# Layer 1 of a gated cross-attention kernel: rows, normed rows and weighed products turned by transposing DMAs instead of TensorE

## The chip, the cores and the metric

One core of a Trainium2 chip runs the whole program. The metric is the device time of one execution in microseconds, as the median of several runs.

## The reference

```python
x = x + tanh(g_xattn[0]) * L0_xattn(layernorm(x), ctx)
x = x + tanh(g_ffn[0])   * L0_ffn(layernorm(x))            # 8 experts, top 2
x = x + tanh(g_xattn[1]) * L1_xattn(layernorm(x), ctx)
x = x + tanh(g_ffn[1])   * L1_ffn(layernorm(x))

def L1_xattn(x, c):        # 16 heads of 64
    q, k, v = x @ Wq / 8, c @ Wk, c @ Wv
    return softmax(q @ k.T) @ v @ Wo

def L1_ffn(x):             # 32 prototypes, rank 16
    dists = sqrt(max(|x|^2 + |p|^2 - 2 x @ prototypes.T, 0))
    w = softmax(-dists / max(|temp|, 0.1))
    topw, topi = top_k(w, 2);  topw = topw / sum(topw)
    return sum over both: topw * (A[topi] @ (B[topi] @ x) + bias[topi])
```

`x` is 64 x 256 x 256, the context 64 x 77 x 256, both f32. Everything from the third line of the sum on is "layer 1" here.

## The kernel before

The program prepares keys and values, runs layer 0's attention, layer 0's experts on the first 1024 rows, and then layer 1 in `attention_ffn_phase`. Only this last phase changes. It goes through 64 batches (`NB`) of 256 rows, two tiles of 128 rows each (`TPB`), so 128 tiles. Each matrix product in f16 is made of three matmuls, by `matmul3`: high x high, high x low, low x high. A high half is a ScalarE copy to f16 and a low half is a VectorE subtraction from the f32 value (`split_hi`, `split_lo`).

Each engine runs the same `body(i, u, j)` for batch i, with two iterations h, one per tile t = 2i + h. It is a software pipeline written out by hand: an iteration does the scores of tile t, the exp of t-1, the normalising of t-2, the turning of probabilities and the attention product of t-3, the second norm `yn` of t-4, the products `low` (with the prototypes' distances) of t-5, the weights of t-6, and the weighing `hw`, its turning and the last product `ffn` of t-7. `LAG` is 7: SyncE stores tile t-7 in iteration t. The queries of batch i+1 are made in four groups (`prep`) inside batch i, and its normed rows `xn` were made at the end of batch i-1.

TensorE's order in an iteration: turn the probabilities' group 0; group 1; the 48 score matmuls; group 2; in the first tile turn `xn` (four turns of 128x128 in f32); turn `hw` (four); `low` (12); turn `wsel`; the attention product (30 matmuls); a group of queries (12 matmuls); turn `yn` (two); `ffn` (13). All PSUM results but the scores go through five banks in a fixed ring (`Ring`, `uses`, `freed`); an entry of it waits for the reader of the entry five before.

VectorE's order: the sums' reciprocals; low halves of the probabilities; low half of `xnT` in the first tile; maxima of the scores; statistics of the rows two batches ahead; low half of `hwT`; the shifted scores; distances; the residual; `bn_stats`; a query's low half; averages `mv2`; `pick`; low half of `ynT`; `wsel`; the two nearest prototypes; the last addition to `y`.

GpSimd's order: in the second tile `deviation` (four steps on [128, 2]: add eps, negate the mean, a power of -0.5, a product); `deviation2` for tile t-4 (the same on [128, 1]); `weigh`; `length2` (three steps); `top_weights` (eight small steps, three of them powers); `normalise` (two products that write `pn`); `softmax_sums` (three adds).

SyncE issues every load and store of the phase in one order, and waits in that order. For a batch these are the keys (308 KB), the rows `x` (256 KB), two loads and two stores of a tile (128 KB each), and the values: two loads `vo_front` and eight `vo_back` of 13 partitions each.

Of the kernel before, what the change touches and what calls it, by code (L numbers as in the profile page):

```python
# [708 lines left out]
def attention_ffn_phase(nc, ctx, psum, const, src, src_rows, dst, keys, values, wq, score_scale, ffn, experts):  # L709
# [27 lines left out]
    VALUE_LOADS = 16 * (2 + MAIN)  # L737
# [6 lines left out]
    LAG = 7  # L744
# [3 lines left out]
    SUM_STEPS, LN2_STEPS, TOP_STEPS = 2, 2, 5  # L748
# [7 lines left out]
    xnT = pair("xnT", [P, DC, SEQ])  # L756
# [4 lines left out]
    idle, numbers = sb("idle", [P, 1]), sb("numbers", [P, 5])  # L761
# [17 lines left out]
    xnT_hi, xnT_ready, q_hi, q_ready = sem("xnT_hi"), sem("xnT_ready"), sem("q_hi"), sem("q_ready")  # L779
# [6 lines left out]
    ln2_sums, ln2_stats, ln2_step, ln2_done, ysq_done, yn_ready = (  # L786
        sem("ln2_sums"), sem("ln2_stats"), sem("ln2_step"), sem("ln2_done"), sem("ysq_done"), sem("yn_ready"))
    ln2_inverse = sem("ln2_inverse")
    ynT_hi, ynT_ready, dots_read = sem("ynT_hi"), sem("ynT_ready"), sem("dots_read")
# [4 lines left out]
    low_ready, hw_ready, hwT_hi, hwT_ready, wselT_hi, wselT_ready, out_ready = (  # L794
        sem("low_ready"), sem("hw_ready"), sem("hwT_hi"), sem("hwT_ready"), sem("wselT_hi"), sem("wselT_ready"),
# [33 lines left out]
    def norm_apply(i, u):  # L829

        need(act, ln_done, i + 1)
        for a in range(TPB):
# [27 lines left out]
    class First:  # L860
# [29 lines left out]
        def scalar_rows(self):  # L890
            act.wait_ge(early_full, 1)
            act.activation(xnT[0][:, :, :], parted(rows_bank, DC), ACT.Copy).then_inc(xnT_hi, 1)

        def vector_rows(self):
            dve.wait_ge(xnT_hi, 1)
            nc.vector.tensor_tensor(xnT[1][:, :, :], parted(rows_bank, DC), xnT[0][:, :, :], ALU.subtract)\
                .then_inc(xnT_ready, 1)

        def tensor_rows_taken(self):
            pe.wait_ge(xnT_ready, 1)  # L900

        def tensor_query(self, n):
            need(pe, q_ready, n - 1)
            for b in range(QB):
                at = (n * QB + b) * P
                for c in range(DC):
                    last = matmul3(nc, query_bank(n)[:, b * SEQ:(b + 1) * SEQ], [w[:, c, at:at + P] for w in wq],
                                   [a[:, c, :] for a in xnT], c == 0, c == DC - 1)
# [16 lines left out]
    k_sb.append(sb("k1", [P, BLK, KEYS, 2], F16))  # L925
    vo_front = [sb(f"vo_front{p}", [P, MAIN, 2, D], F16) for p in range(2)]
# [13 lines left out]
    ynT = pair("ynT", [P, DC, P])  # L940
# [10 lines left out]
    hwT = pair("hwT", [P, LC, P])  # L951
# [4 lines left out]
    def prep_uses(h, part):  # L956

        at = {(0, 1): [("xnT", 0)], (0, 2): [("q", 0)], (0, 3): [("q", 1)], (1, 0): [("q", 2)], (1, 2): [("q", 3)]}
        return at.get((h, part), [])

    def uses(i):

        names = []
        for h in range(TPB):
# [6 lines left out]
            names += prep(1)  # L971
            names += of(7, [("hwT", h)])
# [4 lines left out]
            names += of(4, [("ynT", h)])  # L977
            names += of(7, [("ffn", h)])
# [5 lines left out]
    def freed(i, use):  # L984
# [7 lines left out]
        if what == "xnT":  # L992
            return xnT_ready, i + 2
# [4 lines left out]
        if what == "ynT":  # L998
            return ynT_ready, t - 3
        return {"hwT": hwT_ready, "wselT": wselT_ready, "ffn": out_ready}[what], t - 6  # L1000
# [16 lines left out]

    def prob_of(u, h, age):
# [4 lines left out]
    last_keys = lambda tile: tile[:, H * FRONT:SC].rearrange("p (h k) -> p h k", h=H)  # L1023
# [5 lines left out]
    def _(sp):  # L1029
# [11 lines left out]
        def load_values(i, u, j):  # L1041
# [4 lines left out]
            for n in range(MAIN):  # L1046
                sp.dma_start(vo_back[p][n * BACK:(n + 1) * BACK, :, :, :], values_back(batch_at(i), n)).then_inc(vo_in[p], 16)
# [5 lines left out]

        def body(i, u, j):
            if live(i + 1, NB):
                load_keys(i + 1, *ahead(u, j, 1))
            for h in range(TPB):
                t = i * TPB + h - LAG
                if live(t, NT):
# [3 lines left out]
                if live(i * TPB + h - 2, NT):  # L1063
                    load_rows(i * TPB + h - 2, *place(2, u, h, j))
                if h == 0 and live(i + 3, NB):
                    load_x(i + 3, *ahead(u, j, 3))
# [21 lines left out]
    def _(pool):  # L1088
# [15 lines left out]
        def normalise(t, h, u):  # L1104
# [4 lines left out]
            for keys_of, first, end in ((first_keys, 0, FRONT), (last_keys, FRONT, KEYS)):  # L1109
                last = pool.tensor_tensor(keys_of(pn[h]), e[:, :, first:end],  # L1110
                                          rsum[h][:, :].unsqueeze(2).broadcast_to([P, H, end - first]), ALU.mult)
            last.then_inc(pn_ready, 1)

        def deviation2(t, h):

            need(pool, ln2_stats, t + 1)
            need(pool, yn_ready, t)
            step = Steps(pool, ln2_step, t, LN2_STEPS)
            vare_ready = pool.tensor_tensor(vare2[:, :], mv2[:, 1:2], eps[:, :], ALU.add)
            pool.tensor_scalar(minus_mean2[:, :], mv2[:, 0:1], -1.0, None, ALU.mult)  # L1120
            step(vare_ready)
            step(pool.tensor_tensor(rstd2[:, :], vare2[:, :], numbers[:, 0:1], ALU.pow))
# [1773 lines left out]
```

## Time and profile before

| what | value |
|---|---|
| median of 3 runs | 3064.41 us (3062.23 to 3066.16) |
| the profiled execution's own time | 3063.96 us |
| its span, first to last instruction | 3062.1 us |
| mean granted TensorE clock | 0.977 |
| busy in the span: TensorE, VectorE | 2839.0 us (93%), 2538.6 us (83%) |
| busy in the span: GpSimd, ScalarE | 2160.7 us (71%), 1832.1 us (60%) |
| first and last score maximum of layer 1 begin at | 1469.0 us, 2997.0 us |

An engine's busy time is the time that at least one of its instructions covers; matmuls overlap one another, so their pace is read from their starts and not from their durations. In a row of the timeline the first number is the start in microseconds from the span's start, the second the length.

### The profile page before, as it was taken

The page shows a single profiled execution, that of the slowest core. Times are in us where ns is not written, and L with a number is a line of the kernel's source. Part 1 is how long each engine was busy: PE and PEld are TensorE (multiplying, and loading weights), DVE is VectorE, ACT ScalarE, POOL GpSimd, SP SyncE. Part 2 cuts the span into 40 slices and gives each one's busy share as a digit, 9 for nine tenths or more (in the row PEclk, how much of TensorE's full clock was granted, in tenths as well). Part 3 has the DMA queues.
Part 4 walks back from the last instruction along what each step waited for, and adds up shares of the span by engine and source line. Part 5 has one row for each costly group of instructions (what it writes and reads, how often), then busy time and mean ns, then how long its engine had stood idle before and what let it go on. Part 6 is the DMA issues. An engine that isn't in the chain of part 4 may idle for free.

```text
span 3062.1 us, 98061 instructions
## 1 busy us (share of the span) xinstructions
PE 2839.0 (93%) x32554; PEld 2276.5 (74%) x32554; DVE 2538.6 (83%) x6189; ACT 1832.1 (60%) x3605; POOL 2160.7 (71%) x3859
## 2 busy tenths in 40 slices
PE   4888896899999999789899999999999999999997
PEld 2444444677777877557688888888888888888886
DVE  6877786788888888675799999899888899998986
ACT  2666765678777777575455555555555555555553
POOL 3893000666676666554599888888888888888887
PEclk7999998899999999899999999999999999999999
DMA  5987666233232333631544444444444444444431
GB/s 151 363 338 293 240 242 259 68 83 91 79 93 76 90 83 82 236 97 42 121 105 110 115 97 102 97 95 97 106 92 105 99 98 101 95 97 106 104 89 44
DMA packets 367616, 388.73 MB, mean 127 GB/s; under 512 B 118432, under 2 KB 341264, under 8 KB 362320
## 3 DMA queue, kind: packets, MB, share of 16 engines
q1 hardware_dynamic: 346960, 335.42, 39.5%
q0 software_dynamic: 7328, 23.40, 2.5%
q10 hardware_dynamic: 12960, 25.23, 2.2%
q8 instruction: 203, 3.33, 0.5%
q14 instruction: 165, 1.35, 0.2%
HBM read 235.08 MB, written 148.83 MB: 125 GB/s over the span
## 4 chain that ended last, share of the span: by engine, by line
PE 40%; DVE 6%; issue 3%; POOL 2%; ACT 1%; DVEq 0%; POOLq 0%; ACTq 0%
PE banks L150 11%; PE banks L152 11%; PE banks L151 11%; PE banks L1308 3%; PE banks L1293 2%; DVE a_probT_lo L1395 1%; PE banks L1340 1%; DVE a_pick L1518 1%; ACT a_qT_hi L1197 1%; DVE a_y L1537 1%; DVE a_rsum L1407 1%; DVE a_wsel L1527 0%; PE banks L1363 0%; PE banks L1355 0%; ACT a_ynT_hi L1197 0%
## 5 line engine op out<-in xcount | busy, mean ns | idle before, releaser
L1197 ACT ACTIVATE a_qT_hi<-banks 128x512 f16<-128x512 f32 x252 | 150.5, 597 | 692.5 <-PE banks L152 692.5
L383 POOL TENSOR_TENSOR a_probT_lo<-a_expT,a_probT_hi 128x512 f16<-128x512 f32 x256 | 291.3, 1159 | 218.9 <-ACT a_probT_hi L466 218.9
L459 ACT ACTIVATE a_expT<-banks,a_top,w_score_scale 128x512 f32<-128x512 f32 (+1 forms) x384 | 272.5, 710 | 153.5 <-PE banks L550 145.4
L1110 POOL TENSOR_TENSOR a_pn<-a_prob,a_rsum 128x1024 f32<-128x1024 f32 (+1 forms) x256 | 310.2, 1233 | 4.5 <-DVE a_rsum L1409 4.3
L150 PE MATMUL banks<-a_xnT_hi,w_q_hi 128*128 128x256 f16 x1024 | 280.8, 274 | 4.7 <-DVE a_xnT_lo L1393 3.0
L150 PE MATMUL banks<-a_vo_front,a_probT_hi 128*128 128x256 f16 x1024 | 279.2, 273 | 2.7 <-DVE a_probT_lo L1395 2.6
L152 PE MATMUL banks<-a_xnT_hi,w_q_lo 128*128 128x256 f16 x1024 | 280.2, 274 | 0.0
L151 PE MATMUL banks<-a_xnT_lo,w_q_hi 128*128 128x256 f16 x1024 | 280.1, 274 | 0.0
L152 PE MATMUL banks<-a_vo_front,a_probT_lo 128*128 128x256 f16 x1024 | 279.2, 273 | 0.0
L151 PE MATMUL banks<-a_vo_front,a_probT_hi 128*128 128x256 f16 x1024 | 279.1, 273 | 0.0
L1395 DVE SCALAR_TENSOR_TENSOR a_probT_lo<-banks,a_probT_hi 128x512 f16<-128x512 f32 (+1 forms) x384 | 212.1, 582 | 34.8 <-ACT a_probT_hi L1197 33.5
L1393 DVE TENSOR_TENSOR a_qT_lo<-banks,a_qT_hi 128x512 f16<-128x512 f32 x252 | 172.5, 684 | 69.9 <-ACT a_qT_hi L1197 66.2
L550 PE MATMUL banks<-ident,a_shifted 128*128 128x128 f32 (+1 forms) x1280 | 204.3, 283 | 5.3
L1197 ACT ACTIVATE a_probT_hi<-banks 128x512 f16<-128x512 f32 (+1 forms) x384 | 193.7, 523 | 25.1 <-PE banks L1308 25.1
L2264 DVE SCALAR_TENSOR_TENSOR kv_vo_out<-banks,kv_vo_out 128x512 f16<-128x512 f32 (+1 forms) x312 | 191.3, 679 | 15.3 <-ACT kv_vo_out L2162 15.3
L1308 PE MATMUL banks<-ident,a_pn 128*128 128x128 f32 (+1 forms) x1280 | 196.9, 277 | 2.4 <-issue 2.4
L659 DVE TENSOR_TENSOR a_shifted<-banks,a_smax 128x1024 f32<-128x1024 f32 (+1 forms) x256 | 192.1, 792 | 3.8
L2162 ACT ACTIVATE kv_vo_out<-banks 128x512 f16<-128x512 f32 (+1 forms) x312 | 172.4, 601 | 26.5 <-DMA vo<-kv_vo_out 20.1
L649 DVE TENSOR_REDUCE a_smax<-banks 128x16 f32<-128x1232 f32 x128 | 183.7, 1435 | 1.9 <-PE banks L536 1.5
L550 PEld LDWEIGHTS banks<-ident,a_shifted 128*128 128x128 f32 (+1 forms) x1280 | 142.6, 140 | 43.8 <-ACT a_expT L459 18.2
L1222 ACT ACTIVATE a_prob<-a_prob,w_score_scale 128x1232 f32<-128x1232 f32 x128 | 169.4, 1324 | 0.5 <-DVE a_prob L1425 0.5
L1099 POOL TENSOR_TENSOR a_half<-a_prob 128x512 f32<-128x512 f32 x128 | 165.6, 1294 | 3.8 <-ACT a_prob L1222 3.8
(383 smaller groups left out, 10314.5 us busy)
## 6 DMA issues: line engine op xcount, KB each, us to landing
vo<-kv_vo_out SPq DMA_DIRECT2D x38, 2048.0 KB, 7.0
a_vo_front<-vo SPq DMA_DIRECT2D x128, 512.0 KB
kt<-kv_k_out ACTq DMA_DIRECT2D x9, 2560.0 KB, 14.9
a_k<-kt SPq DMA_DIRECT2D x64, 308.0 KB, 3.5
kv_raw_e<-in_L_ffn_w POOLq DMA_DIRECT2D x16, 1024.0 KB, 9.0
a_x<-in_x SPq DMA_DIRECT2D x64, 256.0 KB, 2.9
a_y<-in_x SPq DMA_DIRECT2D x64, 256.0 KB, 2.8
x<-a_y SPq DMA_DIRECT2D x64, 256.0 KB, 2.9
```

Source lines behind the costliest of these rows:

```text
L150: nc.tensor.matmul(out, lhs[0], rhs[0], start=start, stop=False)
L151: nc.tensor.matmul(out, lhs[0], rhs[1], start=False, stop=False)
L152: return nc.tensor.matmul(out, lhs[1], rhs[0], start=False, stop=stop)
L383: pool.tensor_tensor(probT[b][1][:, first:end, :], expT[b][:, first:end, :], probT[b][0][:, first:end, :], ALU.subtract).then_inc(prob_rea ...
L459: act.activation(expT[1 - h][0:rows, first:end, :], bank, ACT.Exp, bias=top[0:rows, 0:1], scale=weights["score_scale"][0:rows, 0:1]).then_ ...
L550: last = nc.tensor.transpose(bank[0:rows, c * P:(c + 1) * P], shifted[1 - h][:, place:place + rows], ident[:, :])
L659: last = nc.vector.tensor_tensor(shifted[h][:, cols].rearrange("p (r h k) -> p r h k", r=TILES, k=end - first), held_scores[:, :, :, first ...
L1110: last = pool.tensor_tensor(keys_of(pn[h]), e[:, :, first:end], rsum[h][:, :].unsqueeze(2).broadcast_to([P, H, end - first]), ALU.mult)
L1197: act.activation(out, bank[:, 0:cols].rearrange("p (c s) -> p c s", c=out.shape[1]), ACT.Copy, scale=scale)\
L1308: last = nc.tensor.transpose(bank[0:rows, c * P:(c + 1) * P], pn[1 - h][:, place:place + rows], ident[:, :])
L1395: nc.vector.scalar_tensor_tensor(out=lo, in0=bank, scalar=scale, in1=hi, op0=ALU.mult, op1=ALU.subtract)\
L2264: nc.vector.scalar_tensor_tensor(out=vo_out[q][0:m, placed(b), 1, :], in0=product_banks(g, c, b, m), scalar=1.0 / OUT_TOP, in1=vo_out[q][0 ...
```

## The change

- The normed rows `xn` of a batch, `yn` of a tile and `hw` of a tile are split into halves *before* they are turned: a ScalarE copy to f16 (`rows_high`, `normed_high`, `weighed_high`) into `xn_parts`, `yn_parts`, `hw_parts`, and a subtraction for the low half, on GpSimd for the rows and `yn` (`rows_low`, `normed_low`), on VectorE for `hw` (`weighed_low`). SyncE then turns both halves by one transposing DMA each time (`turn_rows`, `turn_normed`, `turn_weighed`). TensorE's turns of the three, and the splits behind them, go.
- `xnT`, `ynT` and `hwT` become two buffers each. `ffn` of a tile moves one iteration later and ahead of `low` on TensorE, and `LAG` is 8.
- The numbers of both norms move from GpSimd to ScalarE, as Ln, Exp(-0.5 x), products and a square (17 instructions a batch). The two last steps of the weights move from GpSimd to VectorE, as a reciprocal and a product.
- The eight `vo_back` loads become one, of 104 partitions, with the heads in another order, for which `normalise` writes the last 13 keys by key and not by head.
- SyncE's order in an iteration is new.

```diff
-    VALUE_LOADS = 16 * (2 + MAIN)
+    VALUE_LOADS = 16 * (2 + 1)
-    LAG = 7
+    LAG = 8
...
-            for n in range(MAIN):
-                sp.dma_start(vo_back[p][n * BACK:(n + 1) * BACK, :, :, :], values_back(batch_at(i), n)).then_inc(vo_in[p], 16)
+            sp.dma_start(vo_back[p][:, :, :, :], values_back(batch_at(i))).then_inc(vo_in[p], 16)
...
+        def begin(done, value):
+            if not isinstance(value, int) or value > 0:
+                sp.wait_ge(done, value)
+                sp.sem_inc(turn_begun, 1)
...
+        def turn_rows(i, u, j):
+            p, _ = turn(u, j, 2)
+            begin(xn_lo, i)
+            begin(q_ready, (i - 1) * QU)
+            sp.dma_start_transpose(xnT[p][:, :, :], xn_parts[:, :, :, :].rearrange("p a s d -> p (a s d)")).then_inc(xnT_in[p], 16)
+        def turn_normed(t, p):
+            begin(yn_lo, t + 1)
+            begin(low_ready, (t - 1) * LU)
+            sp.dma_start_transpose(ynT[p][:, :, :], flat(yn_parts[:, :, :])).then_inc(ynT_in[p], 16)
+        def turn_weighed(t, p):
+            begin(hw_lo, t + 1)
+            begin(out_ready, t - 1)
+            sp.dma_start_transpose(hwT[p][:, :, :], flat(hw_parts[:, :, :])).then_inc(hwT_in[p], 16)
...
             for h in range(TPB):
+                if h == 0 and live(i + 1, NB):
+                    turn_rows(i + 1, *ahead(u, j, 1))
                 t = i * TPB + h - LAG
+                if live(i * TPB + h - 2, NT):
+                    load_rows(i * TPB + h - 2, *place(2, u, h, j))
+                if h == 0 and live(i + 3, NB):
+                    load_x(i + 3, *ahead(u, j, 3))
+                if live(i * TPB + h - 7, NT):
+                    turn_weighed(i * TPB + h - 7, 1 - h)
+                if live(i * TPB + h - 4, NT):
+                    turn_normed(i * TPB + h - 4, h)
                 if live(t, NT):
                     slot = (TPB * u + h - LAG) % SLOTS
                     need(sp, out_ready, t + 1)
                     sp.dma_start(dst[tile_at(t)], y_sb[slot][:, :]).then_inc(out_done[slot], 16)
...
+        def rows_low(i):
+            need(pool, xn_hi, i)
+            pool.tensor_tensor(xn_parts[:, :, 1, :], xn[:, :, :], xn_parts[:, :, 0, :], ALU.subtract).then_inc(xn_lo, 1)
+        def normed_low(t):
+            need(pool, yn_hi, t + 1)
+            pool.tensor_tensor(yn_parts[:, 1, :], yn[:, :], yn_parts[:, 0, :], ALU.subtract).then_inc(yn_lo, 1)
...
+        def norm2_log(t):
+            need(act, ln2_stats, t + 1)
+            act.activation(minus_mean2[:, :], mv2[:, 0:1], ACT.Copy, scale=-1.0)
+            act.activation(vare2[:, :], mv2[:, 1:2], ACT.Ln, bias=eps[:, 0:1]).then_inc(ln2_log, 1)
+        def norm2_root(t):
+            need(act, ln2_log, t + 1)
+            act.activation(rstd2[:, :], vare2[:, :], ACT.Exp, scale=-0.5).then_inc(ln2_root, 1)
...
+        def weighed_high(t, u, h, j):
+            need(act, hw_ready, t + 1)
+            if live(t - 1, NT):
+                earlier, times = turned_place(8, u, h, j)
+                need(act, hwT_in[earlier], (times + 1) * 16)
+            act.activation(hw_parts[:, 0, :], hw[:, :], ACT.Copy).then_inc(hw_hi, 1)
...
+        def weighed_low(t):
+            need(dve, hw_hi, t + 1)
+            nc.vector.tensor_tensor(hw_parts[:, 1, :], hw[:, :], hw_parts[:, 0, :], ALU.subtract).then_inc(hw_lo, 1)
+        def nearer_weight(t):
+            need(dve, more_ready, t + 1)
+            nc.vector.reciprocal(wtop[:, 0:1], more[:, :]).then_inc(first_weight, 1)
+        def farther_weight(t):
+            need(dve, first_weight, t + 1)
+            nc.vector.tensor_tensor(wtop[:, 1:2], late[:, :], wtop[:, 0:1], ALU.mult).then_inc(wtops_ready, 1)
...
+                if live(t - 8, NT):
+                    turned, times = turned_place(8, u, h, j)
+                    need(pe, hwT_in[turned], (times + 1) * 16)
+                    need(pe, wselT_ready, t - 7)
+                    bank = bank_for(i, ("ffn", h))
```

## Rows read from the trace of the kernel before

**Rows 1.** Busy time by stretch; behind the clock the DMA share and GB/s.

```profile
1800.00:2800.00 1000.00, 990.47 (x11946) 870.55 (x11944) 896.67 (x2614) 527.75 (x1105) 887.59 (x1878) 1.00 0.43 100
```

**Rows 2.** Turns of hw in that stretch; then all score maxima (min/median/max, first and last start).

```profile
L1340 PE MATMUL banks<-ident,a_hw 128*128 128x128 f32 x328 | 49.3, 273 | 0.0
...
L1414 DVE TENSOR_REDUCE a_smax<-banks x128: 1109/1110/1112, 1469.0 to 2997.0; 128x12 f32<-128x924 f32 x128
```

**Rows 3.** TensorE's timeline, a first tile's iteration and part of the second's.

```profile
2253.91 1.04 PE L1308 MATMUL banks<-ident,a_pn 128*128 128x128 f32 x8
2254.88 0.25 PE L1293 MATMUL banks<-a_k,a_qT_hi 64*128 64x77 f16 x4
...
2255.88 0.42 PE L1308 MATMUL banks<-ident,a_pn 128*104 128x128 f32 x2
2256.15 0.60 PE L1269 MATMUL banks<-ident,a_xn 128*128 128x128 f32 x4
2256.58 0.60 PE L1340 MATMUL banks<-ident,a_hw 128*128 128x128 f32 x4
2257.29 0.30 PE L150 MATMUL banks<-w_downT_hi,a_ynT_hi 128*128 128x288 f16 x1
...
2262.18 0.27 PE L150 MATMUL banks<-a_xnT_hi,w_q_hi 128*128 128x256 f16 x1
...
2263.49 0.38 PE L1363 MATMUL banks<-ident,a_yn 128*128 128x128 f32 x2
...
2270.13 0.60 PE L1340 MATMUL banks<-ident,a_hw 128*128 128x128 f32 x4
2270.56 0.29 PE L150 MATMUL banks<-w_downT_hi,a_ynT_hi 128*128 128x288 f16 x1
```

**Rows 4.** VectorE's timeline in the same batch.

```profile
2254.19 0.42 DVE L1393 TENSOR_TENSOR a_ynT_lo<-banks,a_ynT_hi 128x256 f16<-128x256 f32 x1
...
2258.07 0.68 DVE L1393 TENSOR_TENSOR a_xnT_lo<-banks,a_xnT_hi 128x512 f16<-128x512 f32 x1
2258.67 1.11 DVE L1414 TENSOR_REDUCE a_smax<-banks 128x12 f32<-128x924 f32 x1
...
2261.03 0.66 DVE L1393 TENSOR_TENSOR a_hwT_lo<-banks,a_hwT_hi 128x512 f16<-128x512 f32 x1
```

**Rows 5.** The smallest VectorE and ScalarE instructions (busy us, mean ns).

```profile
L2464 DVE TENSOR_TENSOR w_low_scale<-w_low_unit,gates 128x1 f32<-128x1 f32 x1 | 0.2, 159 | 0.0
...
L1614 ACT ACTIVATE gates<-gates 128x4 f32<-128x4 f32 x1 | 0.2, 205 | 1.8 <-DMA gates<-in_g_ffn 1.8
```

**Rows 6.** A VectorE instruction with both inputs in SBUF; both engines' timeline around one.

```profile
L1555 DVE TENSOR_TENSOR a_first_x<-a_first_x,a_first_bias x8: 415/866/995, 1475.4 to 1800.1; 128x256 f32<-128x256 f32 x8
...
1604.16 1.06 POOL L1155 TENSOR_TENSOR a_hw<-a_low,a_wsel 128x512 f32<-128x512 f32 x1
1604.55 0.94 DVE L1555 TENSOR_TENSOR a_first_x<-a_first_x,a_first_bias 128x256 f32<-128x256 f32 x1
1605.17 0.37 POOL L1128 TENSOR_TENSOR a_inv<-a_rstd 128x1 f32<-128x1 f32 x1
```

**Rows 7.** GpSimd by line (busy us, mean ns), then its timeline.

```profile
L383 POOL TENSOR_TENSOR a_probT_lo<-a_expT,a_probT_hi 128x512 f16<-128x512 f32 x256 | 291.3, 1159 | 218.9 <-ACT a_probT_hi L466 218.9
...
L1122 POOL TENSOR_TENSOR a_rstd<-a_vare,a_numbers 128x1 f32<-128x1 f32 x128 | 72.8, 569 | 0.0
...
2260.10 2.42 POOL L1110 TENSOR_TENSOR a_pn<-a_prob,a_rsum 128x1024 f32<-128x1024 f32 x2
```

**Rows 8.** SyncE's timeline; then a load by size and median us to landing.

```profile
2271.22 7.92 SPq L1047 DMA_DIRECT2D a_vo_back<-vo  x8
...
a_x<-x SPq DMA_DIRECT2D x64, 256.0 KB, 3.1
```

**Rows 9.** ScalarE: a query's high half by line, and xn in the timeline.

```profile
L1197 ACT ACTIVATE a_qT_hi<-banks 128x512 f16<-128x512 f32 x252 | 150.5, 597 | 692.5 <-PE banks L152 692.5
...
2277.61 1.09 ACT L833 ACTIVATE a_xn<-a_x,a_shift,a_rstd 128x256 f32<-128x256 f32 x2
```

More of the change, by code:

```diff
@@ L778, in attention_ffn_phase @@
         sem("ln_sums"), sem("ln_stats"), sem("ln_step"), sem("ln_done"), sem("xn_ready"))
-    xnT_hi, xnT_ready, q_hi, q_ready = sem("xnT_hi"), sem("xnT_ready"), sem("q_hi"), sem("q_ready")
+    first_hi, first_turned = sem("first_hi"), sem("first_turned")
+    xn_hi, xn_lo, q_hi, q_ready = sem("xn_hi"), sem("xn_lo"), sem("q_hi"), sem("q_ready")
+    xnT_in, ynT_in, hwT_in = ([sem(f"{n}_in{p}") for p in range(2)] for n in ("xnT", "ynT", "hwT"))
+    turn_begun = sem("turn_begun")
     odd_scored = sem("odd_scored")
@@ L939, in attention_ffn_phase @@
     yn = sb("yn", [P, D])
-    ynT = pair("ynT", [P, DC, P])
+    yn_parts = sb("yn_parts", [P, 2, D], F16)
+    ynT = [sb(f"ynT{p}", [P, 2 * DC, P], F16) for p in range(2)]
     ysq = sb("ysq", [P, TPB])
@@ L950, in attention_ffn_phase @@
     hw = sb("hw", [P, LOW])
-    hwT = pair("hwT", [P, LC, P])
+    hw_parts = sb("hw_parts", [P, 2, LOW], F16)
+    hwT = [sb(f"hwT{p}", [P, 2 * LC, P], F16) for p in range(2)]
     first_x = [sb(f"first_x{n}", [P, D]) for n in range(FIRST_X)]
@@ L997, in freed @@
             return y_ready, t - 2
-        if what == "ynT":
-            return ynT_ready, t - 3
-        return {"hwT": hwT_ready, "wselT": wselT_ready, "ffn": out_ready}[what], t - 6
+        return (wselT_ready, t - 6) if what == "wselT" else (out_ready, t - 7)
     def bodies(eng, body):
@@ L1162, in body @@
                 t = i * TPB + h
[L1163 to L1166 removed]
+                if h == 0 and live(i + 1, NB):
+                    rows_low(i + 1)
                 if live(t - 7, NT):
                     weigh(t - 7, 1 - h)
[L1169 to L1170 removed]
                 if live(t - 6, NT):
                     top_weights(t - 6)
+                if live(t - 4, NT):
+                    normed_low(t - 4)
                 if live(t - 2, NT):
@@ new lines, in rows_high, with normed_high @@
+        def rows_high(i, u, j):
+            p, _ = turn(u, j, 2)
+            earlier, times = turn(u, j, 2, -1)
+            need(act, xn_ready, i + 1)
+            if not isinstance(i, int) or i > 1:
+                act.wait_ge(xnT_in[earlier], (times + (1 if earlier == 1 else 0)) * 16)
+            act.activation(xn_parts[:, :, 0, :], xn[:, :, :], ACT.Copy).then_inc(xn_hi, 1)
+        def normed_high(t, u, h, j):
+            need(act, yn_ready, t + 1)
+            if live(t - 1, NT):
+                earlier, times = turned_place(5, u, h, j)
+                need(act, ynT_in[earlier], (times + 1) * 16)
+            act.activation(yn_parts[:, 0, :], yn[:, :], ACT.Copy).then_inc(yn_hi, 1)
@@ L1348, in body @@
                         for c in range(DC):
-                            last = matmul3(nc, bank[:, 0:cols], [a[:, c, :] for a in ynT],
+                            last = matmul3(nc, bank[:, 0:cols], [ynT[turned][:, s * DC + c, :] for s in range(2)],
                                            [w[:, c, n, 0:cols] for w in ffn["down"]], c == 0, c == DC - 1)
@@ L1358, in body @@
                 prep(2)
-                if live(t - 4, NT):
-                    need(pe, yn_ready, t - 3)
-                    bank = bank_for(i, ("ynT", h))
-                    for c in range(DC):
-                        last = nc.tensor.transpose(bank[:, c * P:(c + 1) * P], yn[:, c * P:(c + 1) * P], ident[:, :])
-                    filled(last, i, ("ynT", h))
-                if live(t - 7, NT):
-                    need(pe, hwT_ready, t - 6)
-                    need(pe, wselT_ready, t - 6)
-                    bank = bank_for(i, ("ffn", h))
-                    for c in range(LC):
-                        matmul3(nc, bank[:, 0:D], [a[:, c, :] for a in hwT], [w[:, c, :] for w in ffn["up"]],
-                                c == 0, False)
-                    filled(nc.tensor.matmul(bank[:, 0:D], wselT[:, :], ffn["bias"][:, :], start=False, stop=True),
-                           i, ("ffn", h))
                 prep(3)
```

220 lines of the change are left out of this document (111 added, 109 removed).

## The prediction

> **What bounds the kernel now.** I read the busy time by stretch first. In the steady part of layer 1, TensorE is busy for 990.5 of 1000 us, VectorE for 896.7, GpSimd for 887.6, ScalarE for 527.8; the DMA engines are busy for 0.43 of the time, and the granted clock is 1.00 [rows 1]. The stretch holds 328 turns of the weighed products, four a tile, so 41 batches: **24.4 us a batch** [rows 2]. Over all 128 tiles the score maxima give (2997.0 - 1469.0) / 127 x 2 = 24.1 us [rows 2]. Per batch VectorE is busy 896.7 / 41 = 21.9 us, GpSimd 21.6, ScalarE 12.9.
>
> Busy TensorE is not needed TensorE, as its matmuls overlap, so I read its timeline next, by starts. Twelve query matmuls take 2263.49 - 2262.18 = 1.31 us, 0.109 each; four turns of xn take 0.43 us, so an f32 turn also costs 0.108; 48 score matmuls take 1.00 us [rows 3]. A batch has 146 f16 matmuls of 256 columns (48 queries, 60 attention, 26 up with bias, 12 down), 12 of 288 columns at about 0.12, 38 turns and two score groups: 15.9 + 1.5 + 4.1 + 2.0 = **23.5 us**. So 0.9 us of a batch is loss between groups; one such place is the turn of hw in the first tile, 0.71 us to the next start where the second tile's takes 0.43 [rows 3]. TensorE is the bound, GpSimd and VectorE are both near behind, and the loss is what three nearly full engines do to each other.
>
> **The change, part by part, for one batch.**
> TensorE loses 4 turns of xn, 2 x 2 of yn and 2 x 4 of hw: 16 x 0.109 = 1.7 us, so its need falls to 21.8. The query matmuls read xnT in two runs of 128 columns instead of one of 256; I take 0 for that. A gain is excluded, as the columns are the same; from above, the eight turns that open a tile take 2254.88 - 2253.91 = 0.97 us, 0.121 each [rows 3], and 48 queries at 0.121 would cost 0.6 us more.
>
> VectorE loses the low half of xnT (0.68) and of ynT (2 x 0.42), of which about 0.08 each overlapped the next instruction [rows 4]: -1.3. The low half of hwT (0.66) becomes one of hw of equal size. A reciprocal and a product of one column, each near the 0.16 of such a product [rows 5], and a wait of `pick` on the engine's own result come to some 0.36 a tile: +0.7. The new low half differs in one thing: both its inputs lie in SBUF. `add_experts` has such an instruction, and it took 415 ns at least and 866 in the median; begun at 1604.55 under GpSimd's product of 1604.16 to 1605.22 it took 0.94, and GpSimd's next step 0.37 instead of 0.19 [rows 6]. So it waits for a running GpSimd instruction. Ends: nothing, or the rest of the longest GpSimd instruction, 1.9 us. At random against GpSimd's instructions it is 0.4 a tile, which I take: +0.8. VectorE comes to 21.9 - 1.3 + 0.7 + 0.8 = **22.1 us**.
> The Trainium skill, "SBUF — State Buffer", section "Who interferes with whom", says that VectorE with two SBUF inputs and a GpSimd instruction that reads SBUF share a port, and the later of them blocks fully. This case's rows agree, and by that rule alone the low half would wait whenever the two meet, which is the second rival below.
>
> GpSimd loses deviation2 (0.57 for the power, near 0.2 for each of its other three steps), length2 (three of 0.2) and two weight steps (a power of 0.57 and one of 0.2) per tile, and deviation (1.3, the same four steps on two columns) per batch: 2 x 2.5 + 1.3 = -6.3. It gains rows_low, priced by the same shape in layer 0 at 1.16, and two of half that size at 0.6 to 0.7 [rows 7]: +2.5. The last keys of pn are written in another order; from nothing to a doubling of the 0.5 that they take a tile; I take nothing, since VectorE and TensorE hide either. GpSimd comes to 17.8 of 22 or more, and is no bound.
>
> ScalarE gains 17 instructions of one or two columns at about 0.2 [rows 5]: 12.9 + 3.5 = 16.4. Its high halves keep their sizes. The cover is 6 us of idle; what can hurt are its new waits, in order, for VectorE's averages and for the transfers' landing. Behind them are the high halves of probT and the exp; the averages end about when the iteration begins, two VectorE steps before their low halves, so I take 0.
>
> SyncE issues eight vo_back loads in 7.9 us; they become one, of 0.4 (a plain load's issue) to 1.6. It gains five transposing transfers: one of 256 KB for the rows, two of 128 KB, two of 256 KB, 1 MB in all. The trace has no such transfer. From below, they cost what a plain 256 KB load does: 3.1 us from issue to landing [rows 8]. From above, they are pushed as small pieces, as vo_back is at 7.9 us for 208 KB [rows 8], which is 9.9 us for 256 KB. Each is one request of 128 partitions, as the plain load is, and vo_back's have 13, so I take a value nearer the low end, 4.5 us. The DMA engines go from 10.5 us a batch (0.43 x 24.4 for 2.44 MB) to about 15: hidden, at that rate.
>
> What is the room for them? The rows are tightest. The last query of a batch ends TensorE's iteration; then come its high half (0.60), xn (1.09) [rows 9], the high half (0.61) and GpSimd's low half (1.16), 3.5 us. TensorE meanwhile does turns, scores, ffn, down, wsel and attention, 0.9 + 0.3 + 1.0 + 1.4 + 1.5 + 0.1 + 3.3 = 8.4 us, before it needs xnT: **4.9 us** for the transfer. The weighed products have 6 to 7: their low half now ends 7.8 us behind the iteration's start (2261.03 + 0.66 - 2253.91 [rows 3, 4]), 7.1 once VectorE's earlier work is less, and TensorE asks for it 2.1 us (first tile of a batch) or 3.5 us (second) into the next iteration of 11. The normed rows have 7 to 9, and queue behind the weighed ones on SyncE. At 4.5 us none is late. On SyncE's queue stand, behind each wait, the tile's store and the next values, both with an iteration to spare.
> LAG 8 puts `ffn` an iteration behind the weighing, where the transfer has its time. At the end that costs an iteration: from the last maximum to the end of the span are 3062.1 - 2997.0 = 65 us for seven [rows 2], 9 us each, and with landing times in the tail I take +10.
>
> **The sum.** The batch is the larger need, VectorE's 22.1, plus the 0.9 lost now: 23.0, against 24.4. I take 60 batches of full work and leave the ramp: 60 x 1.4 = 84, less 10: -74. As VectorE's busy time also holds short waits between dependent steps, I round the batch down to 22.9: 60 x 1.5 - 10 = **-80 us**. The profiled execution took 3063.96 us for a span of 3062.1, within 0.5 of the median of 3064.41: 3064.4 - 80 = **2984**.
>
> **The rivals.**
> 1. TensorE alone stays the bound, and losses shrink as GpSimd gets room: 21.8 + 0.3 = 22.1 a batch, 60 x 2.3 - 10 = -128: 2936. For it: GpSimd's 21.6 of 24.4 was one of the three. Against: VectorE's 22.1. Chance 0.12.
> 2. VectorE's two-input low half meets GpSimd's longest product each time (1.9 us long). In the trace of before, hwT's low half starts at 2261.03 [rows 4], inside that product, which begins at 2260.10 [rows 7]. Cost 1.4 a tile instead of 0.4: VectorE 24.1, batch 24.4: 3064 + 10 = about 3070. Against: GpSimd has 1.8 us less ahead of that product and waits for yn's high half before it. Chance 0.07.
> 3. Slower: the transposing transfers land late. TensorE then waits before the first query of each batch for all beyond 4.9 us, and before ffn beyond 6 to 7. The gain of 1.5 a batch is used up at 4.9 + 1.5 = 6.4 us for 256 KB, twice the plain load; that is the point from which it decides. At the upper end, 9.9 us, the waits are 5.0 + 3.9 + 2.9, or 8 to 12 a batch with part of them covering each other: batch some 31, 60 x 6.6 = +400: 3450. Between, at 7.5 us, +1.5 a batch: 3150. Against: plain transfers of this size land in half the limit. Chance 0.23.
> The Trainium skill is at odds with itself here. "VectorE: DVE Perf Modes", section "The three transpose paths", gives 1309 ns for a DMA transpose of 128x128; eight in a row would be 10.5 us for 256 KB, an estimate by that page that is this rival. "Advanced Engine Details and Errata", section "X-Bar Transpose (TRN2)", says that such transfers are as fast as regular ones, which is my forecast's side. No row here shows which.
> 4. The change does nothing that can be measured: the gain is eaten by half of 2 and of 3 together. Chance 0.05.
> The forecast's own case (batch 22.4 to 23.8) has 0.53, and its own range is 2950 to 3030.
>
> **How the numbers follow.** Case 1 and the forecast are faster: 0.65, and 0.03 of case 2. Within 0.2% (6 us, about what a measurement of this kernel can tell from no change): case 4 and a part of 2, 0.06. Slower: 0.26. The range leaves out 0.03 below (all of case 1 and no drain) at 2930, and what is above 3120, where case 3 has landed at 7 us or later: 0.17.
>
> **What would show it.** In the changed kernel: turns of a_xn, a_yn and a_hw gone from TensorE; query slots still 0.109; a batch of about 22.9 (spacing of a_smax 11.4 a tile); GpSimd near 80% busy, VectorE 95% or more; the hw_parts low half of 0.68 us with a tail to 2; the transfers to xnT, ynT, hwT landing in 3 to 5 us. The prediction is wrong if the list of waits shows TensorE waiting for the landing of xnT, hwT or ynT, or if the transfers take SyncE over 2 us each to issue.

## The result and the profile after

The changed kernel took **3092.03 us** in the median (3091.24 to 3097.04), against 3065.28 us for the kernel before on the same chip: a ratio of 1.0094, 95% interval 1.0076 to 1.0112. It is 0.9% slower. I had forecast 2984 us, faster with a chance of 0.68; the time lies inside my widest range (2930 to 3120 us), but on the wrong side of no change.

The profiled execution took 3097.04 us for a span of 3095.2. First the busy time by stretch (engines PE, PEld, DVE, ACT, POOL, then clock, DMA share, GB/s) and the score maxima of layer 1, which answer to [rows 1, 2].

```profile
1800.00:2800.00 1000.00, 921.54 (x11165) 788.12 (x11163) 936.98 (x2634) 621.80 (x1780) 800.12 (x1095) 1.00 0.67 140
```
```profile
L1504 DVE TENSOR_REDUCE a_smax<-banks x128: 1057/1110/1121, 1466.8 to 3025.4; 128x12 f32<-128x924 f32 x128
```

The maxima give (3025.4 - 1466.8) / 63.5 = **24.5 us a batch**, where [rows 2] gave 24.1 and I forecast 22.9. The loop thus costs 30.6 us more, the time from its last maximum to the end 4.7 us more (69.8 instead of 65.1), and it starts 2.2 us earlier: 33.1 us, the difference of the two spans. TensorE is busy for 921 of 1000 us, VectorE for 937, GpSimd for 800. No engine is full any more, and still the batch is longer. So the next view is the chain that ended last, by engine, of the kernel before and of the changed one.

```profile
PE 40%; DVE 6%; issue 3%; POOL 2%; ACT 1%; DVEq 0%; POOLq 0%; ACTq 0%
```
```profile
PE 18%; DVE 11%; POOL 10%; issue 9%; ACT 2%; DMA 1%; DVEq 0%; SPq 0%; POOLq 0%; ACTq 0%
```

TensorE's share falls from 40% to 18%, and GpSimd's rises from 2% to 10%, although GpSimd has less to do. The waits from 1800 to 2800 us (engine and line, releaser, us, times, longest) say what it waits for:

```profile
POOL a_yn_parts L1166 <- ACT a_yn_parts L1292: 88.6, 41, 2.5
POOL a_hw L1187 <- DVE a_wsel L1634: 71.7, 80, 2.4
...
PE banks L150 <- DVE a_probT_lo L1485: 39.3, 41, 1.4
```

Once a batch, in its second tile, GpSimd stands 2.2 us before `normed_low`, until ScalarE has written the normed rows' high half. ScalarE's and GpSimd's timelines there:

```profile
2210.92 0.60 ACT L1227 ACTIVATE a_qT_hi<-banks 128x512 f16<-128x512 f32 x1 [0.66 <-PE banks L152]
2211.41 0.19 ACT L1257 ACTIVATE a_minus_mean<-a_mv 128x1 f32<-128x1 f32 x1
...
2212.17 1.32 ACT L1317 ACTIVATE a_prob<-a_prob,w_score_scale 128x1232 f32<-128x1232 f32 x1
2213.38 0.20 ACT L1263 ACTIVATE a_rstd<-a_vare 128x1 f32<-128x1 f32 x1
...
2215.61 0.42 ACT L1292 ACTIVATE a_yn_parts<-a_yn 128x256 f16<-128x256 f32 x1
```
```profile
2213.73 0.19 POOL L1180 TENSOR_TENSOR a_more<-a_late,a_numbers 128x1 f32<-128x1 f32 x1
2216.11 0.67 POOL L1166 TENSOR_TENSOR a_yn_parts<-a_yn,a_yn_parts 128x256 f16<-128x256 f32 x1 [2.19 <-ACT a_yn_parts L1292]
2216.74 2.37 POOL L1152 TENSOR_TENSOR a_pn<-a_prob,a_rsum 128x1024 f32<-128x1024 f32 x1
2219.06 0.81 POOL L1154 TENSOR_TENSOR a_pn<-a_prob,a_rsum 128x208 f32<-128x208 f32 x1
```

ScalarE computes the norm's numbers one at a time between a query's high half (which waits for TensorE), the exp of 1.32 us and the probabilities' high halves; the normed rows' high half ends at 2216.03. GpSimd was free at 2213.92. Behind its wait stand the probabilities `pn` and the softmax sums, for which nothing there was missing: they start 2.2 us late.

VectorE, SyncE and the transfers, over the whole span (ns min/median/max; the last three rows end in the median us from issue to landing):

```profile
L1627 DVE TENSOR_SCALAR a_pick<-iota,a_topf,a_wtop x256: 287/301/1245, 1541.0 to 3077.0; 128x32 f32<-128x32 f32 x128
...
L1555 DVE TENSOR_TENSOR a_hw_parts<-a_hw,a_hw_parts x128: 678/786/2198, 1547.9 to 3082.6; 128x512 f16<-128x512 f32 x128
...
L1089 SPq DMA_TRANSPOSE a_hwT<-a_hw_parts x128: 1232/1267/2312, 1549.0 to 3083.5; - x128
...
L1057 SPq DMA_DIRECT2D a_vo_back<-vo x64: 435/591/2133, 1475.4 to 3024.0; - x64
```
```profile
a_ynT<-a_yn_parts SPq DMA_TRANSPOSE x128, 2.3
a_hwT<-a_hw_parts SPq DMA_TRANSPOSE x128, 3.2
a_xnT<-a_xn_parts SPq DMA_TRANSPOSE x63, 3.1
```

The transfers land in 2.3 to 3.2 us. `pick` is 0.30 us in the median and up to 1.25: once a batch it begins just before GpSimd's quarter add ends and then lasts as long as the instruction that GpSimd starts next, `rows_low` of 1.16 us. The chain by line, over the whole span, holds it with as large a share as GpSimd's product `pn`:

```profile
PE banks L150 5%; PE banks L152 5%; PE banks L151 5%; POOL a_pn L1152 2%; PE banks L1409 2%; DVE a_pick L1627 2%; DVE a_smax L1504 1%; POOL a_half L1142 1%; PE banks L1394 1%; POOL a_hw L1187 1%; DVE a_probT_lo L1485 1%; POOL a_pn L1154 1%; DVE a_stats L855 1%; DVE a_prob L1513 1%; POOL a_quarter L1144 1%
```

### The profile page after: what moved, and what is told of

Its sections match the earlier page's. It is cut to its first block, busy times and chain, and to the rows that moved or that the text cites. A ratio compares the mean times of both kernels' runs of the same rounds, so it can differ in the third digit from the quotient of the medians.

```text
span 3095.2 us, 95570 instructions
## 1 busy us (share of the span) xinstructions
PE 2750.9 (89%) x31534; PEld 2160.9 (70%) x31534; DVE 2611.5 (84%) x6254; ACT 1984.6 (64%) x4683; POOL 2033.9 (66%) x2649
## 4 chain that ended last, share of the span: by engine, by line
PE 18%; DVE 11%; POOL 10%; issue 9%; ACT 2%; DMA 1%; DVEq 0%; SPq 0%; POOLq 0%; ACTq 0%
PE banks L150 5%; PE banks L152 5%; PE banks L151 5%; POOL a_pn L1152 2%; PE banks L1409 2%; DVE a_pick L1627 2%; DVE a_smax L1504 1%; POOL a_half L1142 1%; PE banks L1394 1%; POOL a_hw L1187 1%; DVE a_probT_lo L1485 1%; POOL a_pn L1154 1%; DVE a_stats L855 1%; DVE a_prob L1513 1%; POOL a_quarter L1144 1%
## 5 line engine op out<-in xcount | busy, mean ns | idle before, releaser
L150 PE MATMUL banks<-a_xnT,w_q_hi 128*128 128x256 f16 x1024 | 281.3, 275 | 29.0 <-DVE a_dots L1524 14.8
L152 PE MATMUL banks<-a_xnT,w_q_lo 128*128 128x256 f16 x1024 | 280.6, 274 | 0.0
L151 PE MATMUL banks<-a_xnT,w_q_hi 128*128 128x256 f16 x1024 | 280.5, 274 | 0.0
L1152 POOL TENSOR_TENSOR a_pn<-a_prob,a_rsum 128x1024 f32<-128x1024 f32 x128 | 270.4, 2112 | 5.5 <-DVE a_rsum L1499 5.5
L1187 POOL TENSOR_TENSOR a_hw<-a_low,a_wsel 128x512 f32<-128x512 f32 x128 | 135.4, 1058 | 120.8 <-DVE a_wsel L1634 120.8
L150 PE MATMUL banks<-w_downT_hi,a_ynT 128*128 128x288 f16 (+1 forms) x512 | 144.1, 282 | 57.5 <-DVE a_probT_lo L1485 57.0
L1166 POOL TENSOR_TENSOR a_yn_parts<-a_yn,a_yn_parts 128x256 f16<-128x256 f32 x128 | 86.2, 674 | 144.1 <-ACT a_yn_parts L1292 144.1
```

Source lines behind the costliest of these rows:

```text
L150: nc.tensor.matmul(out, lhs[0], rhs[0], start=start, stop=False)
L151: nc.tensor.matmul(out, lhs[0], rhs[1], start=False, stop=False)
L152: return nc.tensor.matmul(out, lhs[1], rhs[0], start=False, stop=stop)
L1152: pool.tensor_tensor(first_keys(pn[h]), e[:, :, 0:FRONT], rsum[h][:, :].unsqueeze(2).broadcast_to([P, H, FRONT]), ALU.mult)
```

## The experiments

Before the first four runs I held three theories. **A**: VectorE closes the cycle of a batch, through `pick` held up by GpSimd, and through the ring of five banks, in which a query group now takes the bank that the read of the prototype products frees. **B**: the transposing transfers and SyncE's queue. **C**: GpSimd waits, in its own order, for ScalarE. Ratios are to the kernel before on the same chip: runs 1 to 4 had one chip, 5 to 8 a second, 9 to 12 a third, so between these groups the ratios compare better than the microseconds. I held A to be likelier than C.

**1. `rows_low` behind the weighing on GpSimd.**
```
-                if h == 0 and live(i + 1, NB):
-                    rows_low(i + 1)
                 if live(t - 7, NT):
                     weigh(t - 7, 1 - h)
+                if h == 0 and live(i + 1, NB):
+                    rows_low(i + 1)
```


> On GpSimd the low half of the rows (1.16 us) goes behind the weighing instead of ahead of it; nothing else changes. Theory A (the cycle of one batch runs through VectorE, and VectorE's one-source `pick` is held up behind whatever GpSimd starts next): no GpSimd work begins at the end of the quarter add, so the first `pick` of the two tiles drops from about 1.20 us back to 0.30, and 0.6 to 1.3 us go from each of 60 batches: 3015 to 3057 us. Theory B (the transposing transfers and SyncE's queue set the time): the rows' transfer only starts later, so no gain, 3086 to 3110 us. Theory C (GpSimd waits in its own order for ScalarE): the weighing comes 0.5 us earlier but the waits for yn stay, so 3080 to 3092 us.

Measured: 3104.04 us, ratio 1.0117 (1.0101 to 1.0134). `pick` in the stretch, and who waits:
```profile
L1627 DVE TENSOR_SCALAR a_pick<-iota,a_topf,a_wtop x162: 287/299/691, 1804.0 to 2797.5; 128x32 f32<-128x32 f32 x162
```
```profile
POOL a_yn_parts L1166 <- ACT a_yn_parts L1292: 86.7, 40, 2.4
...
PE banks L150 <- DVE a_dots L1524: 38.3, 35, 1.4
```
```profile
L1555 DVE TENSOR_TENSOR a_hw_parts<-a_hw,a_hw_parts 128x512 f16<-128x512 f32 x80 | 115.6, 1446 | 0.0
```
With nothing behind the quarter add the long `pick` is gone, as A had it, but the time got no shorter. This doesn't clear `pick`, because the edit brought two new losses. The weighed products' low half on VectorE now meets GpSimd's product `pn` and lasts 1.45 us in the mean instead of 0.92. VectorE is busy with `pick` and this low half for 4.3 us a batch, against 4.1 in the changed kernel. And TensorE waits 9.8 us in 1000 for the rows' transfer, which comes later. GpSimd's wait for ScalarE stands, and TensorE's wait only changes its name.

**2. The prototype products read first on VectorE.**
```
+                if live(t - 5, NT):
+                    prototype_products(i, t - 5, h)
                 if live(t - 7, NT):
                     weighed_low(t - 7)
                 if live(t, NT):
                     shift_scores(t, h, u)
-                if live(t - 5, NT):
-                    prototype_products(i, t - 5, h)
```


> On VectorE the read of the prototype products (0.23 us) goes ahead of the weighed products' low half and of the subtraction of the maxima (together 2.2 to 2.5 us); nothing else changes. Theory A (with the three turns out of the ring of five banks, the second query group takes the bank that this read frees, and the cycle closes there): TensorE can begin that group up to 2.3 us earlier; part of it is caught by the next wait, so 0.4 to 1.5 us go from each batch: 3000 to 3068 us. Theory B: no change, 3086 to 3098 us. Theory C: no change, 3086 to 3098 us.

Measured: 3089.52 us, 1.0075 (1.0058 to 1.0092), 0.1% below the changed kernel; the intervals overlap. TensorE's wait for the products is gone from the list, and waits for the queries' low halves have taken its place. So this wait alone doesn't set the time. The edit has a price too: the weighed products' low half, now later, lasts 1.49 us in the mean, and `pick` and the low half together take 4.5 us a batch.

**3. Every transposing transfer twice.** The second copy goes to a tile that nobody reads; all waits count both.
```
             sp.dma_start_transpose(hwT[p][:, :, :], flat(hw_parts[:, :, :])).then_inc(hwT_in[p], 16)
+            sp.dma_start_transpose(again["hwT"][p][:, :, :], flat(hw_parts[:, :, :])).then_inc(hwT_in[p], 16)
```


> Each transposing transfer is issued twice, the second time into a tile that nobody reads, and every reader and writer waits for both. This doubles their time on SyncE's queue (1.25 us each) and their bytes, and puts the later landing at 4.5 to 6 us instead of 3.1. Theory A: the transfers lie beside other work, so the time moves by less than 0.5%: 3085 to 3107 us. Theory B (they bound or nearly bound the batch): five more issues of 1.25 us a batch and DMA engines that are busy past 0.95 give 2 to 6 us a batch more: 3200 to 3450 us. Theory C: as A.

Measured: 3197.9 us, 1.0434 (1.0417 to 1.0452): 106 us above the changed kernel, just under B's range and far outside A's and C's.
```profile
1800.00:2800.00 1000.00, 884.70 (x10540) 751.50 (x10538) 885.85 (x2485) 594.98 (x1680) 755.27 (x1031) 0.97 0.94 173
```
```profile
PE banks L150 <- DMA a_hwT_again<-a_hw_parts: 44.4, 27, 2.7
PE banks L150 <- DMA a_xnT_again<-a_xn_parts: 22.8, 23, 2.3
```
Twice the transfers fill the DMA engines to 0.94 and cost 1.7 us a batch. TensorE then waits for landings, which it hardly does in the changed kernel. So the transfers have no room for a second set, but this doesn't make the first the cause. Whether the DMA engines or SyncE's queue (9% of this run's chain, 0% of the changed kernel's) is what runs out, the run doesn't say, as it doubles both.

**4. `normed_low` behind `normalise` on GpSimd.**
```
-                if live(t - 4, NT):
-                    normed_low(t - 4)
                 if live(t - 2, NT):
                     normalise(t - 2, h, u)
+                if live(t - 4, NT):
+                    normed_low(t - 4)
```


> On GpSimd the low half of the normed rows goes behind the probabilities' product instead of ahead of it; nothing else changes. Theory C (GpSimd's order makes it wait 2.2 us a batch for ScalarE's high half, and the probabilities come late by that): most of the 2.2 us goes, 1.5 to 2.2 us a batch: 2960 to 3002 us. Theory A: GpSimd has no full load, and the gain is only that its quarter add ends about 2 us earlier and `pick` then no longer falls between two of its instructions: 0.3 to 1.2 us a batch, 3020 to 3074 us. Theory B: no change or, as the normed rows' transfer starts 2 to 3 us later, slower: 3092 to 3130 us.

Measured: **3045.04 us, 0.9932 (0.9916 to 0.9949)**: faster than both kernels, from one swap.
```profile
PE 26%; DVE 11%; issue 7%; ACT 5%; POOL 1%; DMA 1%; DVEq 0%; SPq 0%; ACTq 0%; POOLq 0%
```
```profile
POOL a_xn_parts L1161 <- ACT a_xn_parts L1284: 84.0, 41, 2.3
POOL a_hw L1187 <- DVE a_wsel L1634: 39.8, 42, 2.0
```
GpSimd leaves the chain (10% to 1%). The time is in A's range and not in C's, and what A foresaw did happen: the longest `pick` in the stretch is 0.50 us. The swap takes away two things at once, the wait of 2.2 us ahead of `pn`, and VectorE's hold-ups by GpSimd: `pick` and the weighed products' low half take 2.9 us a batch instead of 4.1. In run 1 the hold-up only moved from one to the other. How the 47 us (50 by the ratios) divide between the two, no run shows. A new wait of 2.0 us for the rows' high half stands on GpSimd and keeps part of the gain back, as run 5 shows.

**5. ScalarE's rows earlier, on top of run 4.** `norm_apply` and `rows_high` fill a stretch in which ScalarE waited for TensorE.
```
+                if h == 1 and live(i + 2, NB):
+                    norm_apply(i + 2, u + 2)
+                    rows_high(i + 2, (u + 2) % BODIES, j + (u + 2) // BODIES)
                 prep(2)
-                if h == 1 and live(i + 2, NB):
-                    norm_apply(i + 2, u + 2)
-                    rows_high(i + 2, (u + 2) % BODIES, j + (u + 2) // BODIES)
```


> The kernel of the fourth run (normed rows' low half behind the probabilities' product) and, on ScalarE, the rows' normalisation and high half (1.08 and 0.63 us) ahead of the last query block instead of behind it, into a stretch of 3.1 us in which ScalarE waited for TensorE. In the fourth run GpSimd waited 84.0 us in 1000 (2.0 us a batch) for this high half. Theory C (GpSimd's queue closes the cycle of a batch, its waits for ScalarE included): that wait goes and the batch gets shorter by 0.5 to 2.0 us: 2925 to 3015 us. Theory A (VectorE and the ring of banks close it): no more than 0.3 us a batch: 3027 to 3045 us. Theory B (the transfers): no gain, 3040 to 3055 us.

Measured: **3008.7 us, 0.9830 (0.9810 to 0.9851)**, in C's range alone. GpSimd waits for ScalarE no more; its waits are for VectorE's weights' table, and TensorE is busy 962.57 of 1000 us.
```profile
POOL a_hw L1187 <- DVE a_wsel L1634: 112.8, 85, 3.4
...
POOL a_xn_parts L1161 <- issue: 2.4, 1, 2.4
```
GpSimd's waits add up to nearly as much (113 us against 124 in run 4). Which wait it is decides, not their sum: this one stands before the weighing and leaves the product `pn` in time. VectorE's hold-ups hardly change here (`pick` and the low half: 2.9 us a batch in run 4, 2.8 now), so they don't explain the gain of 36 us (31 by the ratios).

**6. `rows_low` behind the weighing, on top of run 4** (the edit of run 1).

> The kernel of the fourth run and, on GpSimd, the rows' low half behind the weighing. Theory C: the weighing (1.06 us) fills half of the 2.0 us wait for ScalarE, 0.3 to 1.0 us a batch: 2985 to 3027 us. Theory A: no change, 3038 to 3052 us. Theory B: the rows' transfer starts no earlier, no gain: 3040 to 3060 us.

Measured: 3029.99 us, 0.9896 (0.9877 to 0.9915): 15 us below run 4 (11 by the ratios), 3 us above C's range and 8 us below A's, so nearer to C. `pick` takes as long as in run 4, 0.33 us in the mean. The same edit gained nothing in run 1, where the other wait still stood and where the low half got longer by 0.53 us a tile (here by 0.07).

**7. The last keys by head again, on top of run 4.** Eight loads of values and `last_keys` as in the kernel before.
```
-            sp.dma_start(vo_back[p][:, :, :, :], values_back(batch_at(i))).then_inc(vo_in[p], 16)
+            for n in range(MAIN):
+                sp.dma_start(vo_back[p][n * BACK:(n + 1) * BACK, :, :, :], values_back(batch_at(i), n)).then_inc(vo_in[p], 16)
```


> The kernel of the fourth run with the last keys laid out by head as in the kernel before: GpSimd writes them in order (0.51 us a tile there, 0.99 us now) and SyncE issues eight loads of values again in place of one. Theory C: GpSimd's queue is shorter by 1.0 us a batch, of which 0.3 to 1.0 us are seen: 2985 to 3027 us. Theory A: less than 0.3 us a batch, 3027 to 3048 us. Theory B: seven more issues on SyncE (about 0.5 us a batch) for nothing: 3045 to 3075 us.

Measured: 3069.62 us, 1.0018 (1.0004 to 1.0032): 25 us slower than run 4, against C and for B.
```profile
L1058 SPq DMA_DIRECT2D a_vo_back<-vo x328: 803/807/1783, 1803.1 to 2784.2; - x164
```
```profile
PE banks L150 <- DMA a_hwT<-a_hw_parts: 24.9, 23, 2.6
...
SPq L1069 <- DVE a_hw_parts L1555: 84.8, 41, 4.4
```
Eight loads hold SyncE for 8 x 0.807 = 6.5 us instead of 0.6. Its own idle time before the weighed products falls from 329.7 us (run 4) to 84.8, the transfers behind the loads come late, and TensorE waits for them. GpSimd's saving (0.99 to 0.70 us a tile) didn't show.

**8. Runs 5 and 7 together.**

> The edits of the fifth and the seventh run together. Theory C: both sources of GpSimd's cycle go, until TensorE (22.7 us busy a batch) is the bound: 22.9 to 23.3 us a batch, 2985 to 3015 us, or 10 to 30 us below the better of the two. Theory A: 3020 to 3045 us. Theory B: 3040 to 3080 us.

Measured: 3035.51 us, 0.9903 (0.9877 to 0.9928): 27 us above run 5, in A's range and in neither of the others. The reason is B's and not A's: SyncE's queue has 9% of the chain, and TensorE waits 21.7 us in 1000 for the weighed products' transfer. It is the price of the eight loads again.

**9. The edit of run 5 on the changed kernel alone.**

> The changed kernel with ScalarE's rows moved ahead of the last query block, as in the fifth run, but with GpSimd's normed low half still ahead of the probabilities' product. In the changed kernel GpSimd waited for the rows' high half 1.0 us in 1000 and for the normed rows' high half 88.6 us. Theory C (what counts is the wait that GpSimd meets first): no gain as long as that other wait stands, 3080 to 3100 us, against the 36 us that the same edit brought on the fourth run's kernel. If the rows' high half were late by itself, the gain would be here as there: 3050 to 3065 us.

Measured: 3089.23 us, 1.0102 (1.0081 to 1.0123), as C has it: no gain while the first wait stands (87.0 us in 1000, 40 times); behind run 4 it was worth 36 us. The long `pick` stands here too (0.60 us in the mean), so this run doesn't separate the two either.

**10. Run 5 with the prototype products first** (the edit of run 2).

> The fifth run's kernel with the prototype products read first, as in the second run. There TensorE waits 8.3 us in 1000 for this read and is busy 962 us. Theory C with TensorE as the next bound: at most 0.2 us a batch, 2996 to 3012 us. Theory A's ring of banks, if it became the bound once GpSimd's queue is free: 0.4 us a batch and more, under 2990 us.

Measured: **3000.1 us, 0.9804 (0.9787 to 0.9822)**, the fastest of all, though its interval meets that of run 5.
```profile
1800.00:2800.00 1000.00, 969.27 (x11976) 851.35 (x11975) 938.92 (x2826) 670.95 (x1908) 855.15 (x1172) 1.00 0.76 151
```
```profile
PE 40%; issue 3%; DVE 3%; POOL 2%; ACT 2%; DMA 1%; SPq 1%; DVEq 0%; POOLq 0%; ACTq 0%
```
```profile
L1504 DVE TENSOR_REDUCE a_smax<-banks x128: 1108/1111/1121, 1460.8 to 2920.7; 128x12 f32<-128x924 f32 x128
```
The chain is TensorE's again, with the 40% of the kernel before, and a batch is (2920.7 - 1460.8) / 63.5 = 22.99 us.

**11. Run 5 with a query's low half behind the picks on VectorE.**
```
-                prep(2)
                 ...
+                prep(2)
                 if live(t - 5, NT):
                     nearest_two(t - 5, h)
```


> The fifth run's kernel; on VectorE the low half of the query block of part 2 goes behind the picks and the weights' table instead of ahead of them. In the fifth run VectorE waited 32.8 us in 1000 for ScalarE's high half there, and GpSimd waited 112.8 us for the weights' table. If a queue through VectorE and GpSimd still sets the batch: 0.3 to 0.8 us a batch, 2960 to 2992 us. If TensorE is the bound (962 of 1000 us busy): within 0.3%, 3000 to 3018 us.

Measured: 3080.31 us, 1.0058 (1.0035 to 1.0081): 72 us slower than run 5, which neither expectation had.
```profile
PE banks L1394 <- DVE a_qT_lo L1483: 62.0, 31, 2.4
```
In run 5 TensorE waited 16.9 us for that low half before the scores. So VectorE's order can be spoilt as well, and a short wait in it can be the right place to stand.

**12. The kernel before with one load of the last keys' values** and `last_by_key`.

> The kernel before with one part of the change: one load of the last keys' values in place of eight, and GpSimd writes those keys' probabilities strided. Nothing is transposed by DMA. Theory C: GpSimd has 1.0 us a batch more where it was busy 887.6 of 1000 us, of which 0.2 to 1.0 us a batch are seen: 3077 to 3127 us. If seven issues less on SyncE's queue were worth something by themselves: 3035 to 3060 us. If both are covered: within 0.2% of the kernel before.

Measured: 3064.38 us, 1.0005 (0.9996 to 1.0015): nothing. With runs 7 and 8, this part of the change is worth something once five transposing transfers share SyncE's queue. (By the code it is the read of the probabilities that is strided; `pn` is written in order. The product takes 0.82 us instead of 0.55.)

## Why the prediction was wrong

**The step that failed** is the price of the new waits. I wrote of ScalarE: "what can hurt are its new waits, in order, for VectorE's averages and for the transfers' landing [...] so I take 0", and of GpSimd that it "is no bound". I looked at what is queued behind ScalarE's waits, and not at who waits in order for ScalarE. I even used GpSimd's wait for yn's high half as an argument against the second rival, and gave it no price. It stands once a batch for 2.2 us ahead of `pn`. Moving `normed_low` from in front of `pn` gave 47 us (run 4). Taking away the next wait of GpSimd for ScalarE gave 36 more, with VectorE's hold-ups unchanged (run 5); the edit of run 6, which fills half of that wait, gave 15. Each of these two edits gave nothing on the changed kernel (runs 9 and 1). So waits that I had put at 0 cost time; but not all of the 47 us need be the wait's, as the next two points say.

**The form of the sum** failed with it: the larger need plus the 0.9 lost now. The loss is no constant. By the busy time, TensorE's idle time went from 0.2 us a batch to (1000 - 921.5) / 40.5 = 1.9 while its need fell. With the order mended the number comes near, 22.99 us a batch in run 10 against 22.9, and 3000 us against 2984. But there TensorE is the larger, with 22.3 us busy against VectorE's 938.92 / 43.5 = 21.6, and not VectorE as in my sum, so this is in part luck.

**TensorE's need: right.** Twelve query matmuls of the changed kernel:
```profile
2207.65 0.28 PE L150 MATMUL banks<-a_xnT,w_q_hi 128*128 128x256 f16 x1 [0.18 <-DVE a_dots L1524]
...
2208.97 0.60 PE L1409 MATMUL banks<-ident,a_pn 128*128 128x128 f32 x4
```
1.32 us for twelve, 0.110 each, as [rows 3] had: reading xnT in two runs costs nothing. In run 10 TensorE is busy 969.27 / 43.5 = 22.3 us a batch, against 24.2 in [rows 1]: 1.9 less, where I said 1.7.

**VectorE: 23.1 us a batch, not 22.1.** (40.5 batches in the stretch.) The weighed products' low half took 0.92 us in the mean there, 0.24 over its shortest of 0.68; I had 0.4 over it. What I missed is `pick`: with a single input in SBUF it too waits for GpSimd, for a mean of 0.62 us instead of 0.30, four times a batch, 1.3 us. This is the second term that I had too small, and it may be part of the cause: put into my sum, 23.1 gives 24.0 us a batch where 24.5 were measured. `pick` lies on the changed kernel's chain, run 1 only moved the hold-up to the low half, and run 4, which gave the gain, brought VectorE to 929.38 / 42 = 22.1. The Trainium skill, "SBUF — State Buffer", section "Who interferes with whom", counts VectorE's two-port modes with a single input among those that take the shared port; the trace agrees (1.22 us, begun 0.05 us before a GpSimd instruction of 1.16 us), though it doesn't show in which mode `pick` ran. I had read only the half on two inputs.

**GpSimd: 19.8 us a batch, not 17.8.** The last keys' product, which I took as free, is
```profile
L1152 POOL TENSOR_TENSOR a_pn<-a_prob,a_rsum 128x1024 f32<-128x1024 f32 x81 | 171.8, 2121 | 0.0
...
L1154 POOL TENSOR_TENSOR a_pn<-a_prob,a_rsum 128x208 f32<-128x208 f32 x82 | 85.7, 1045 | 0.0
```
The last keys' part (L1154) took 0.55 us in the kernel before, so it is 1.0 us a batch more; the first part took 1.92, which is 0.4 more. Some of that is meeting VectorE: in run 5 the two took 0.82 and 1.92 us. The other 0.6 us I haven't split. Run 7 shows that the price of the last keys' part was worth paying.

**Transfers: the mechanism right, the size too high.** 256 KB landed in 3.1 to 3.2 us and 128 KB in 2.3, against 4.5; the stretch's list of waits has no wait of TensorE for a landing, and the third rival fell. The Trainium skill, "Advanced Engine Details and Errata", section "X-Bar Transpose (TRN2)", says that such a transfer is as fast as a regular one, and the trace agrees (3.1 us for a plain 256 KB load, [rows 8]). The estimate of 10.5 us from the Trainium skill, "VectorE: DVE Perf Modes", section "The three transpose paths", did not come true. The other side of it was SyncE's queue, where I gave no price to eight loads beside five transfers: runs 7 and 8 put 25 to 27 us on it. The forecast had the eight go, so this didn't hurt.

**The drain: half of what I took.** 4.7 us instead of 10.

**The second rival** asked for a low half that waits each time; its median is 0.79 us, with a longest of 2.20. Its sum was also wrong: VectorE's 24.1 plus the 0.9 lost is 25.0 us a batch and not 24.4, and some 3110 us. What it had right is that VectorE is held up by GpSimd for more than my forecast's 0.4 us a tile; that this came mostly through `pick` it did not say.

**What stays open.** The 47 us of run 4 aren't split between `pn` coming late and VectorE's hold-ups; a run that takes away one of them and leaves the other is missing. The norms' numbers on GpSimd again, with the rest of the change kept, wasn't tried; so how much of the 2.2 us comes from ScalarE's numbers, and how much from its queue in front of them, isn't split. Nor is it shown which of run 1's two new losses, the longer low half or the later rows' transfer, left it 0.2% above the changed kernel (the intervals overlap).

## What to carry to other kernels

An engine's busy share says nothing about what its order does: before you call it "no bound", list its waits in program order and ask what stands behind each. When work moves to another engine, the wait moves to the old engine's next instruction, and the order can be worth more than the change itself (here one swap turned +0.9% into -0.7%, and two more made it -2.0%). Two waits in a row hide each other: an edit that brings nothing alone can bring 36 us once the first is gone. And before a run without gain clears a suspect, look whether the edit made another instruction longer, as run 1's did.

## What the runs showed of the hardware

A transposing DMA transfer of 256 KB in f16 held SyncE for 1.25 to 1.27 us and landed 3.1 to 3.2 us after its issue. Twice the five of a batch took the DMA share from 0.67 to 0.94. A VectorE instruction with one SBUF input of 32 columns lasted 1.22 us instead of 0.30 when it began 0.05 us before a GpSimd instruction ended and another of 1.16 us followed, and 0.29 where none followed (run 1). A load of 26 KB held SyncE for 0.81 us, with the transposing transfers (run 7) and without them (the kernel before); one of 208 KB in place of eight held it for 0.59 us with them and 0.44 without (run 12).
